# A layer norm, attention and gated FFN kernel on 8 cores: whole R, K, V blocks, and another order in the first stage

## What is computed

```
z  = layernorm(x)                      # x: 4 x 4096 x 1024, f32
q, k, v = z @ Wq, z @ Wk, z @ Wv       # 1024 -> 64
att = softmax(q @ k.T, axis=1)         # over the rows i of q, for each key
x  = x + tile(att @ v, 16)
z  = layernorm(x);  zp = z shifted down by one row
xr = mu_r*z + (1-mu_r)*zp;  xk = mu_k*z + (1-mu_k)*zp
x  = x + sigmoid(xr @ W_r.T) * (square(relu(xk @ W_k.T)) @ W_v.T)
```

## Time and profile before

| | |
|---|---|
| median of 3 runs | 394.92 us (394.86 to 396.29) |
| profiled execution | 394.16 us, span of its slowest core 392.6 |
| spans of the cores | 387.2 to 392.6 us |
| busy, share of the span: TensorE, VectorE, ScalarE, POOL | 80%, 56%, 58%, 28% |
| stages: first and stream to 196; layer norm 2 to 209 | FFN from there to the end |

### The profile page before, as it was taken

One profiled execution on the slowest core, in us unless ns is written; L12 is line 12 of the kernel. 1 busy time (PEld: TensorE's weight loads), 2 busy tenths in 40 slices (PEclk: granted clock), 3 DMA queues, 4 the chain that ended last, 5 costly groups with the idle time before them and its releaser, 6 DMA issues.

```text
span 392.6 us, 6263 instructions; the slowest of 8 cores (387.2 to 392.6 us)
## 1 busy us (share of the span) xinstructions
PE 312.4 (80%) x1931; PEld 144.2 (37%) x1953; DVE 221.1 (56%) x442; ACT 227.5 (58%) x355; POOL 108.8 (28%) x158
## 2 busy tenths in 40 slices
PE   0477976695878767776587996999989998998994
PEld 0333332231224434442253442444434443443441
DVE  3687789237235731111179988579277927682045
ACT  1342289989889999999947267104831275113610
POOL 2787447607303885058500021001000000000000
PEclk9997798866695888887558899999999999999999
DMA  7998357797597779992002014031312223130014
GB/s 207 295 326 290 107 147 188 144 288 104 99 169 201 237 175 190 196 232 108 1 3 53 2 31 76 9 153 56 70 37 110 107 40 68 53 160 2 0 55 161
DMA packets 42369, 48.60 MB, mean 124 GB/s; under 512 B 33248, under 2 KB 33504, under 8 KB 41952
## 3 DMA queue, kind: packets, MB, share of 16 engines
q1 hardware_dynamic: 41472, 41.44, 37.3%
q0 software_dynamic: 864, 6.75, 10.5%
HBM read 38.68 MB, written 8.39 MB: 120 GB/s over the span
## 4 chain that ended last, share of the span: by engine, by line
PE 49%; ACT 18%; DVE 15%; issue 11%; DMA 3%; POOL 1%; SPq 1%; DVEq 0%; ACTq 0%; POOLq 0%
PE F L1080 13%; PE F L1063 11%; PE F L1044 9%; PE F L885 6%; ACT Prot L1150 5%; ACT junkL L1150 5%; PE tf L826 5%; ACT junk L1150 4%; DMA xst<-x_in 3%; DVE xr L665 3%; DVE dxk L675 3%; ACT P L1150 3%; PE acc L898 2%; PE tf L862 1%; DVE bnst L490 1%
## 5 line engine op out<-in xcount | busy, mean ns | idle before, releaser
L885 PE MATMUL F<-qk 64*128 64x512 bf16 x136 | 59.2, 456 | 34.5 <-ACT Prot L1150 11.0
L1044 PE MATMUL F<-wr,xr 128*128 128x512 bf16 x251 | 58.1, 387 | 8.3 <-DVE xr L665 5.5
L1185 ACT ACTIVATE rr<-F 128x1024 bf16<-128x1024 f32 x16 | 16.4, 1025 | 82.2 <-PE F L1044 57.1
L1063 PE MATMUL F<-dxk,wk 128*128 128x512 bf16 x250 | 55.6, 379 | 1.8 <-DVE dxk L675 1.5
L1080 PE MATMUL F<-wv,ka 128*128 128x512 bf16 x251 | 55.6, 379 | 0.3
L889 PE MATMUL F<-qk 64*128 64x512 bf16 x120 | 54.8, 474 | 0.0
L1150 ACT ACTIVATE P<-F,negm 128x1024 bf16<-128x1024 f32 (+1 forms) x40 | 37.2, 948 | 19.6 <-PE F L885 17.4
L1150 ACT ACTIVATE junk<-F,negm 128x1024 bf16<-128x1024 f32 x32 | 39.9, 1258 | 3.0 <-PE F L889 3.0
L1150 ACT ACTIVATE junkL<-F,negm 128x1024 bf16<-128x1024 f32 x32 | 40.0, 1287 | 0.0
L1044 PEld LDWEIGHTS F<-wr,xr 128*128 128x128 bf16 x256 | 25.2, 100 | 40.0 <-issue 12.1
L780 DVE TENSOR_TENSOR tmp<-F,rr 128x1024 f32<-128x1024 f32 x15 | 18.4, 1225 | 36.9 <-PE F L1080 36.0
(11 more groups left out here) (104 smaller groups left out, 444.4 us busy)
## 6 DMA issues: line engine op xcount, KB each, us to landing
xst<-x_in SPq DMA_DIRECT2D x32, 512.0 KB, 7.8
x<-x_in SPq DMA_DIRECT2D x16, 512.0 KB, 5.5
y_out<-x SPq DMA_DIRECT2D x15, 512.0 KB, 2.7
wr<-wr_in POOLq DMA_DIRECT2D x1, 2048.0 KB, 16.3
wk<-wk_in POOLq DMA_DIRECT2D x1, 2048.0 KB, 17.8
wv<-wv_in POOLq DMA_DIRECT2D x1, 2048.0 KB, 21.5
y_out<-x SPq DMA_DIRECT2D x2, 256.0 KB, 2.6
wqk<-wqk_in POOLq DMA_DIRECT2D x1, 256.0 KB, 8.9
```

The lines of the kernel that those rows point to most:

```text
L885: t.matmul(f[:, 0:512], qk2[0:64, kt * 128:(kt + 1) * 128], qk1[0:64, i0:i0 + 512], start=True, stop=True, skip_group_check=True, tile_pos ...
L1044: ins = t.matmul(f[:, hh * 512:(hh + 1) * 512], xr[:, ct, j * 128:(j + 1) * 128], wr[:, ct, hh * 512:(hh + 1) * 512], start=(ct == 0), sto ...
L1063: ins = t.matmul(f[:, dd * 512:(dd + 1) * 512], wk[:, ct, dt * 128:(dt + 1) * 128], dxk[:, q % 2, ct, :], start=(ct == 0), stop=(ct == CT ...
```

## The change

Four things, without a change in what is computed.

1. FFN order: R, K, V of a block whole and in turn (`FSEQ`, TensorE's and ScalarE's loops). V(q,0) waits for the squares one by one, a quarter each.
2. Stage one: z of tiles 5 and 11 is ScalarE's (`AZT`), tile 5 between its fourth and fifth tile copy, tile 11 behind its fourth exp; POOL makes -mean * rstd for them. `z_done(i)` gives the semaphore to wait for. VectorE's list is reordered: the steps of a chunk stand ahead of the statistics of later tiles. TensorE's list too; QK from chunk 1 on and all VP come in two halves with one unit between (`QK2`, `VP2`), and products of the identity that nobody reads stand in the waits: 14, 10 and 6 by 256 columns before QK(0), 4 before QK(1), 8 before QK(3).
3. LN2GRP is tiles 3 to 7, 8 to 15, 0 to 2. The first group waits for the first of three copies of the attention's output. In block 0 the second group's statistics come before `ln2_x1(5)`.
4. `ln2_x1` of the fifth tile comes behind the second mix.

```diff
-        LN2GRP = [(3, 10), (10, 16), (0, 3)]
+        LN2GRP = [(3, 8), (8, 16), (0, 3)]
...
-            FSEQ += [("R", q, j) for j in range(1 if q else 0, 4 if q < 3 else 3)]
-            FSEQ += [("K", q, k_) for k_ in range(4)]
-            FSEQ += [("R", q + 1, 0) if q < 3 else ("R", 3, 3)]
-            FSEQ += [("V", q, j) for j in range(4)]
+            FSEQ += [(kind, q, i) for kind in "RKV" for i in range(4)]
...
@@ gpsimd
                 scale(2 * h, 2, h)
+                if 2 * h + 1 in AZT:
+                    i = 2 * h + 1
+                    g.tensor_tensor(nmr1[:, i:i + 1], nmean[:, i:i + 1], rstd[:, i:i + 1],
+                                    ALU.mult).then_inc(G_NM, 1)
                 apply(2 * h)
-                apply(2 * h + 1)
+                if 2 * h + 1 not in AZT:
+                    apply(2 * h + 1)
@@ vector: the whole list is, up to chunk 3's steps
+ stats(0..7) qk_evac(0) stats_a(8) sw_evac(0) stats_b(8) mx(0) stats(9) stats(10) stats(11)
+ qk_evac(1) t_evac(8) sw_evac(1) mx(1) t_evac(9) stats(12) t_evac(10) t_evac(11) stats(13)
+ qk_evac(2) stats_a(14) sw_evac(2) mx(2) stats_b(14) stats(15) v_evac(0) t_evac(12) t_evac(13)
+ vt_evac(0) stats(16) t_evac(14) t_evac(15) stats(17) qk_evac(3) stats_a(18) sw_evac(3) mx(3)
+ stats_b(18) stats(19) stats(20) v_evac(1) stats(21) vt_evac(1) stats(22) ...
...
-            v.wait_ge(A_TOK, 2)
+            v.wait_ge(A_TOK, 1)
...
             mix_r(c_blk(0), 128, 0, 0)
-            ln2_x1(X1SEQ[4])
             v.wait_ge(A_T2, 2)
             mix_d(c_blk(0) + 128, 128, 128, 0, 2)
             mix_r(c_blk(0) + 128, 128, 128, 0)
+            ln2_x1(X1SEQ[4])
...
+                    v.wait_ge(A_TOK, 3)
+                    ln2_stats(1)
                     ln2_x1(5)
                     ln2_x1(6)
-                    v.wait_ge(A_TOK, 3)
-                    ln2_stats(1)
+                    ln2_shift(1)
                     ln2_x1(7)
-                    ln2_shift(1)
@@ tensor
+            def QK2(n):
+                QK(n, 0, 4)
+                scores(1)
+                QK(n, 4, CT)
+  order: warm_id(14) T0 T1 warm_id(10) T2 T3 warm_id(6) QK(0) T4 T5 SW0 T6 MX0 scores(1) T7 scores(1)
+  warm_id2(4) QK2(1) scores(1) T8 SW1 T9 MX1 T10 scores(2) T11 scores(1) QK2(2) scores(2) SW2 MX2
+  scores(1) VP2(0) scores(2) T12 scores(1) T13 VT0 scores(2) T14 scores(1) T15 warm_id2(8) QK2(3)
+  scores(1) SW3 MX3 scores(2) VP2(1) scores(3) VT1 scores(5) QK2(4) scores(2) SW4 MX4 scores(6)
+  QK2(5) scores(2) SW5 MX5 scores(1) VP2(2) scores(2) VT2 scores(6) QK2(6) scores(2) SW6 MX6
+  scores(2) QK2(7) scores(2) SW7 MX7 scores(1) VP2(3) scores(1) VT3
...
@@ V(q, j)
-                if j == 0:
-                    t.wait_ge(A_KA, 4 * q + 4)
...
+                    if j == 0 and i % 4 == 0:
+                        t.wait_ge(A_KA, 4 * q + dt // 2 + 1)
@@ scalar
+            def apply(i):
+                sc.wait_ge(G_NM, AZT.index(i) + 1)
+                if i >= 8:
+                    sc.wait_ge(P_T, i - 7)
+                sc.activation(zst[:, i % 8, :], xst[:, i % 8, :], AF.Identity,
+                              bias=nmr1[:, i:i + 1], scale=rstd[:, i:i + 1]).then_inc(A_Z, 1)
```

More of the change, by code:

```diff
@@ L139, in build_program @@
         rstd = e(nc.sbuf_tensor("rstd", [128, TT], F32))
+        nmr1 = e(nc.sbuf_tensor("nmr1", [128, TT], F32))
         so = e(nc.sbuf_tensor("so", [128, TOWN], F32))
@@ L294, in build_program, with z_done @@
         block = e(nc.Block())
+        def z_done(i):
+            if i in AZT:
+                return A_Z, AZT.index(i) + 1
+            return G_Z, i + 1 - sum(a < i for a in AZT)
         def own_p(kt):
@@ L824, in QK @@
                     t.wait_ge(V_MX, n)
-                for ct in range(CT):
+                for ct in range(a, b):
                     ins = t.matmul(tf[0][:, :], wqk[:, ct, :],
@@ L854, in MX, with VP @@
                 ins.then_inc(P_MX, 1)
-            def VP(sc):
+            def VP(sc, a=0, b=CT):
                 if sc == 0:
                     t.wait_ge(D_WV, 16)
-                t.wait_ge(V_SW, 2 * sc + 2)
-                for ct in range(CT):
+                t.wait_ge(V_SW, 2 * sc + 2 if sc else 3)
+                for ct in range(a, b):
                     for h in range(2):
@@ L911, in scores, with warm_id, warm_id2, VP2 @@
                     begun += 1
-            t.wait_ge(D_ID, 16)
+            def warm_id(n):
+                for i in range(n):
+                    t.matmul(F[1][:, 0:256], ident, idsw[:, :], start=True, stop=True,
+                             skip_group_check=True)
+            def warm_id2(n):
+                t.wait_ge(V_MX, 3 if n == 8 else 1)
+                for i in range(n):
+                    t.matmul(tf[0][:, 0:256], ident, idsw[:, :], start=True, stop=True,
+                             skip_group_check=True)
+            t.wait_ge(D_ID, 16)
+            warm_id(14)
+            def QK2(n):
+                QK(n, 0, 4)
+                scores(1)
+                QK(n, 4, CT)
+            def VP2(sc):
+                VP(sc, 0, 4)
+                scores(1)
+                VP(sc, 4, CT)
             T(0)
             T(1)
+            warm_id(10)
             T(2)
             T(3)
+            warm_id(6)
             QK(0)
@@ L950, in _ @@
             T(15)
-            scores(2)
-            QK(3)
-            scores(2)
+            warm_id2(8)
+            QK2(3)
+            scores(1)
             SW(3)
@@ L1070, in V @@
             def V(q, j):
-                if j == 0:
-                    t.wait_ge(A_KA, 4 * q + 4)
-                    if q == 0:
-                        t.wait_ge(D_WV2, 16)
+                if q == 0 and j == 0:
+                    t.wait_ge(D_WV2, 16)
                 f_free("V", q, j)
@@ L1101, in _ @@
             warm(1)
-            for j in range(4):
-                R(0, j)
             for q in range(4):
+                for j in range(4):
+                    R(q, j)
                 for k_ in range(4):
                     K(q, k_)
-                if q < 3:
-                    R(q + 1, 0)
-                else:
-                    R(3, 3)
                 for j in range(4):
@@ L1152, in exps @@
                               ).then_inc(A_EXP, 1)
-            for i in range(NA):
-                t_evac(i)
-            for u_ in range(NU):
+            def apply(i):
[4 more added lines that the diff above has]
+                              bias=nmr1[:, i:i + 1], scale=rstd[:, i:i + 1]).then_inc(A_Z, 1)
+            for i in range(4):
+                t_evac(i)
+            apply(5)
+            for i in range(4, NA):
+                t_evac(i)
+            for u_ in range(4):
+                exps(u_)
+            apply(11)
+            for u_ in range(4, NU):
                 exps(u_)
@@ L1208, in _ @@
             ln2_apply(4)
-            for j in range(4):
-                sig(0, j)
             for q in range(4):
+                for j in range(4):
+                    sig(q, j)
                 nx = [x1_n(q + 1, j) - 1 for j in range(4)] if q < 3 else []
```

140 lines of the change are left out of this document (67 added, 73 removed).

## The result

The changed kernel takes 398.2 us (median of 5 runs, 397.88 to 399.12) where the one before takes 396.23 (5 runs, 394.86 to 396.49): a ratio of 1.009, interval 1.0064 to 1.0116. Ratios and intervals here leave out executions in which the cores of one die ran at a lower clock than the others, so this ratio is not that of the two medians, which is 1.005. By the interval the change is slower by 2.5 to 4.6 us; forecast was 387.3, range 382 to 393. The profiled execution has a span of 396.3 (392.6 before); the other cores have 392.4 to 396.2.

What follows compares the result with a forecast made beforehand. No engine bounds the whole span: ScalarE's exps bound 117 to 196 us, waits at projections before, TensorE the FFN. Terms -5.0 - 1.2 + 3.0 - 4.4 = -7.6 from 394.16 give 386.6, plus 0.76 for the median 387.3; range 382 to 393.

Steps and rivals of the forecast that it cites:

- Chunk steps first: Stage one, VectorE and TensorE order: fifth exp at about 36.4, later tiles hardly delayed; 1 us gain taken for z19.
- the rival called slower: Stage one: VectorE's chunk-first order makes tiles late, TensorE stands at QK(4), QK(7); tile 31 at 111.6 means 398.3 us; chance 0.07.
- The prediction's own slow case: Stage one with slow projections: z of tile 15 at 51.3 and of tile 19 at 65.3, nearly no gain.
- Halved projections: Stage one: halves no longer drain ScalarE's exps, opening waits of 0.91, 1.67, 1.66, 1.38 us and QK(3)'s to be gained.
- Early exps: Stage one, ScalarE: fifth exp at about 36.4 (was 40.27), sixth at 37.1 (was 46.33), twentieth unit over some 6 us sooner.
- the stream meets the tiles: Stage one: QK(4) and QK(7) wait for transposed tiles, limiting the gain; exps still end 5.0 us earlier.
- Identity products: TensorE's waits before QK(0), QK(1), QK(3): cost 0, at most 0.9 us; QK(0) at full clock ends at 21.8, not 23.5.
- the case that gave 6.3 for stage one: TensorE in stage one: short bursts of identity products suffice to lift the clock; stage one then gives 6.3 us.
- Identity: ScalarE's z of tiles 5 and 11: no table change, cost 0; otherwise two table loads put the fifth exp back 1.5 us.
- Into the FFN and the regrouping: Layer norm 2 and block 0: shorter first group gives -1.2 us, z of tile 8 waiting for its new group costs +3.0.
- Later blocks: FFN after block 0: TensorE's stalls before R(2,0), R(3,0), K(3,0) and separate tails go, -4.4 us; V(1,3) just covered.
- the sum -5.0 - 1.2 + 3.0 - 4.4: Whole kernel: exps' end, start of layer norm 2, block 0, later blocks; -7.6 us in all.

Runs made afterwards that it cites:

- e3: The changed kernel with VectorE's statistics of tiles 8, 9 and 12 to 20 moved ahead again, about as in the kernel before: 392.33 us, ratio 0.9932 to the kernel before.
- e8: e1 with QK(4) to QK(7) in halves, one unit between: 391.77 us, ratio 0.9931 to the kernel before.
- e10: e9 with QK(4) to QK(7) in halves, one unit between: 385.39 us, ratio 0.9757 to the kernel before.
- e7: e3 with statistics of tiles 26, 27 ahead of QK(5)'s copy and two units between halves from chunk 4 on: 396.87 us, ratio 1.0074 to the kernel before.
- e9: e6 with x loads of tiles 26 to 31 and statistics of 26 to 29 earlier: 386.19 us, ratio 0.9789 to the kernel before.
- e4: The changed kernel without its 42 identity products: 397.8 us, ratio 1.0082 to the kernel before.
- e6: e5 with ln2_x1 of the fifth tile also back ahead of the second mix: 385.41 us, ratio 0.9783 to the kernel before.
- e1: Stage one of the kernel before, layer norm 2 and FFN of the changed kernel: 391.19 us, ratio 0.9915 to the kernel before.
- e5: e1 with the statistics groups, their waits and VectorE's block 0 order of the kernel before: 385.65 us, ratio 0.9795 to the kernel before.

## Why the prediction was wrong, step by step

**The step that failed is "Chunk steps first", with its price.** It priced the statistics behind the chunk steps at z15 49.5 to 51.3 and z19 61.6 to 65.3 and took 1 us of gain. Measured: z15 at 53.97 (before 50.23), z19 at 67.57 (before 63.98), later than the late end of both ranges. The chain by hand gave each statistics operation its own duration and let VectorE work through. It left out that an engine in order also inherits the waits: for tile 11's transpose until 39.41 ahead of the statistics of 13, 3.08 us for QK(2) ahead of those of 14, 1.17 for QK(3) ahead of 18. QK(2) ran wholly at the 1.2 GHz spacing, 1.87 + 1.89 us and a unit between (granted clock 0.50), where it took 2.25 before. It also let every transpose land in about 3 us; tile 19's took 6.2. e3, which changes nothing but this order, gives 6.2 us back.

**What follows from it** is the rival called slower, which had 0.07: TensorE stands at QK(4), then at QK(7); tile 31 lands at 110.98, where 111.6 was written for 398.3 us, and the time is 398.2. The path is that rival's; the match to 0.1 us is luck in part, as tile 31 came 5.4 late and not 6.0 and the FFN gave back 2.0 and not 2.6. The prediction's own slow case ended at z19 65.3, and it leaned to a faster one. The evidence against that was in the earlier trace rows: VectorE idle 8.71 us before QK(5)'s copy and POOL 13.35 behind it, parking of the same kind on the kernel before. But it read all 13.35 as parking: the x of tile 26 landed only at 81.8, 2.1 us before that copy, so there the load held POOL for most of it.

**Halved projections.** "Holds up to 2.2 us of units, so a QK no longer drains it": wrong at the 1.2 GHz spacing. After has 1.15 at QK(5)'s second half and 1.41 + 1.11 at QK(6), where one gap of 1.66 or 1.67 was. A half takes 1.9 us and one unit between gives ScalarE 1.1. In e8 three gaps shrink and two new ones come, without a gain in time; in e10, with the tiles early too, the same three gaps almost go and the fourth, at QK(5), grows. With two units between (e7) the gaps at the halves of QK(4) to QK(6) are 0.64 us at most.

**Early exps.** Fifth at 38.01 for 36.4, sixth at 38.69 for 37.1: right in kind, 1.6 late. The step from there to "some 6 us sooner" at the end was wrong even without the late tiles: in e3 4.2 us of lead at 47 us are 0 at 190. In e3 QK(4), QK(6) and QK(7) each wait for a transpose (1.00, 1.73 and 1.48 us), so the stream can't keep a lead gained ahead of them. No run puts e9's earlier loads into this stage one, so whether the lead would then last is not shown. The prediction saw it ("the stream meets the tiles") and yet booked 5.0, by way of a QK(5) at 76.8, which came at 85.37.

**Identity products, Identity.** Cost 0: right. Gain at QK(0): 1.4 us shorter, ending at 23.3 for 21.8. With 30 products behind each other and transposes between, the granted level did change, so the case that gave 6.3 for stage one had its premise at QK(0) and not at QK(2). The 4 and 8 ahead of QK(1) and QK(3) changed nothing: both ran at the same spacing without them (e4). The Trainium skill, "TensorE: Matmul & The Clock Gate", section "Part 1: The HAM clock gate (the "warmup" mystery)", has half rate as the default that sustained activity lifts; the spacing of QK(0) with them (2.18 us) and without them (3.57) agrees. ScalarE's Identity brought no table load: the trace has the one at 1.47 and the next at 201.02, behind the exps. By this the trace agrees with the Trainium skill, "ScalarE: Activation LUTs", section "Table sets: the hidden batching unit".

**Into the FFN and the regrouping.** The start of layer norm 2: -1.2 forecast; the first z starts 7.1 us behind the exps' end, 8.4 with the old groups (e6): -1.3. Fourth mix_d: it waited for the transpose, as written (1.23 us). ScalarE's wait for the statistics: about 8 us forecast, 7.73 measured; POOL's power for 8 columns 2.58 for 3.2. K(1,0) relative to the exps' end: +1.8 forecast (3.0 less 1.2), +2.2 measured. Right, and by luck: it is a sum of two edits of opposite sign that the prediction did not price apart, -3.4 by the new order and +5.7 by the groups (e1, e5, e6). Nor did it have a term for the lower clock behind V(0,0)'s waits, 2.3 us. Seen apart, it would have said that the regrouping is a loss.

**Later blocks.** From K(1,0) to the last V's start: 101.1 before, 97.0 after, -4.2 for -4.4. No wait of TensorE behind 276: right. VectorE's products held V by 0.3 us at most (V(1) took 14.25 us for 13.98).

So the sum -5.0 - 1.2 + 3.0 - 4.4 measured about +5.7 for the first term and -2.0 for the three others together.

## What to carry to other kernels

When a list of an in-order engine is rearranged, chain the waits it inherits, not only the durations: work whose data is there must not stand behind a step whose producer is late, and e7 shows that the reverse (a step that is ready behind work whose data is late) costs as much. A lead in a stream was mostly gone at the end where the last gates of its inputs had not moved (e3), and moving the last gate alone brought nothing (e9): so start from the last gate and go back, and count both. And price edits one by one even when only their sum is asked: here the FFN order alone is worth 2.2%, and the regrouping and the first stage that came with it took 1.3% and 1.7% away.
